# The end of a graph network kernel: gate written in place in PSUM, last weights loaded whole and split early, last tile in two pieces

## The chip, the cores and the metric

One core of a Trainium2 chip. The metric is device time in microseconds (us), the median of the runs shown. The core has five engines with queues of their own, which wait for each other by semaphores: TensorE (PE, matmuls; its weight loads are listed as PEld), VectorE (DVE), ScalarE (ACT), GpSimd (POOL) and SyncE (SP, which here issues all transfers). SBUF is the on-chip memory of 128 partitions, PSUM the eight banks of 512 fp32 columns into which PE writes.

## The reference

625 nodes with 1024 features, 20,000 edges of 8 types. A graph attention layer, a residual and a layer norm give x1; a relational layer with a gate, a residual and a second layer norm follow. What matters here is the end of the second layer:

```python
u = _rgcn(x, edge_index, edge_type, weight, root, bias)      # x @ root + bias + sum over r of mean_r @ weight[r]
z = jnp.concatenate([u, x], axis=1) @ w_gate + b_gate        # w_gate: 2048 x 1024
h = jnp.tanh(u) * z + x * (1.0 - z)
return h                                                     # and outside: layernorm(x + h)
```

With h rewritten, x + h = 2x + (tanh(u) - x) * z, and this is how both kernels compute it.

## The kernel before

The nodes are cut into five tiles of 128 rows (`NT`, the last has 113), the features into eight chunks of 128 (`KT`) and two halves of 512 columns (`H2`). All products are done in split precision: each fp32 operand is a high part (rounded to fp32r) and a low part (what is left), and each product is three matmuls, high x high, low x high, high x low. So 8 chunks x 5 tiles x 3 = 120 matmuls of 512 columns make one product, called a segment. Segments are numbered: `SEG_Z` (x1's part of z), `SEG_U` and the following 18 (root and the eight relations, two halves each), and then four for u's part of z, of which `SEG_G` is the left half's last one and `SEG_G + 1` the right half, of which all chunks use u.

Weights come chunk by chunk through a ring of four buffers (`RING`): SP loads `w_raw`, ACT rounds it to `w_hi`, POOL subtracts to get `w_lo`, and PE multiplies. `w_used` and `u_ready` tell ACT that a slot is free again. In the loop over relations this runs a few chunks ahead of PE.

The end: for `SEG_G - 1` and `SEG_G` PE goes chunk by chunk, all five tiles per chunk (`product_item`), and in the first two chunks of each it transposes u (`turn_u`), which ACT (`turned_u`) and DVE split into `M_hi[1]` and `M_lo[1]`. These are the transposed u of four chunks each. POOL meanwhile computes `xf` = x1 from its two parts. The last segment goes tile by tile instead, all eight chunks of a tile in turn, so that each tile is ready early; for this all eight chunks of the weights must be there at once. They are put into the memory of `M_hi[0]` and `M_lo[0]` (`last_w`), which is free when `SEG_G - 1` has been used. Their raw parts still come through the ring of four.

ACT then computes tanh of u in place, POOL subtracts xf from it (`minus_x`), and DVE runs `gate` for each tile and half: z += the product (L928), z *= tanh(u) - x (L931), u = 2 xf + z (L932), statistics (L933). In the second half each tile is then normalized: statistics aggregated (L940), square root on ACT (L653), reciprocal (L942), scaling (L943), and SP sends the tile out. The banks of the last segment are 5, 6, 7, 0, 1 for tiles 0 to 4 (`last_bank`), those of `SEG_G` 0 to 4, so tiles 3 and 4 wait for drained banks. The order on each engine is the order in which the code is written.

Of the kernel before, what the change touches and what calls it, by code (L numbers as in the profile page):

```python
# [5 lines left out]
def gat_rgcn_kernel(nc, dst_cols, src_cols, type_cols, dst_units, xT, x, weights, a, bias, b_gate, counts_dram, out):  # L6
    f32 = mybir.dt.float32
    f32r = mybir.dt.float32r
# [42 lines left out]
    GB = 3  # L51
    SUMS = 2 * KT

    def rows(t):
        return P if t < NT - 1 else N - P * (NT - 1)
# [4 lines left out]
    with ctx:  # L60
        def sem(name):
            return ctx.enter_context(nc.semaphore(name))

        def sb(name, shape, dt, where=ctx):
            return where.enter_context(nc.sbuf_tensor(name, shape, dt))
# [14 lines left out]
        stats = sb("stats", [P, NT, 2, 6], f32)  # L80
        y_sum = sb("y_sum", [P, NT], f32)
# [52 lines left out]
        with ExitStack() as late:  # L134
            x1_hi = sb("x1_hi", [P, NT, D], f32r, late)
            x1_lo = sb("x1_lo", [P, NT, D], f32r, late)
            u = sb("u", [P, NT, D], f32, late)
            z = sb("z", [P, NT, D], f32, late)
# [3 lines left out]
            with ExitStack() as agg:  # L142
                C_hi = sb("C_hi", [P, NT, NP], f32r, agg)
            xf = sb("xf", [P, NT, D], f32, late)

        g_parts = [m[:, :, :].rearrange("p a b -> p (a b)") for m in (M_hi[0], M_lo[0])]

        def last_w(low, k):
            return g_parts[low][:, k * H2:(k + 1) * H2]
# [93 lines left out]
        d_done = sem("d_done")  # L243
# [21 lines left out]

        ALL = KT * NT
# [28 lines left out]
        def _(sp):  # L295
# [75 lines left out]
            for n in range(SEG_U + 2 * R, SEG_G + 2):  # L371
                load_ahead(n, last=n == SEG_G + 1)
# [11 lines left out]
        def _(pool):  # L384
# [17 lines left out]
            def last_chunk(k):  # L402
                pool.wait_ge(w_hi_done, 8 * (SEG_G + 1) + k + 1)
                pool.tensor_tensor(last_w(1, k), w_raw[k % RING][:, :], last_w(0, k).bitcast(f32),
                                   ALU.subtract).then_inc(w_lo_done, 1)

            def minus_x(t):
                r = slice(0, rows(t))
                pool.wait_ge(tanh_done, t + 1)
                pool.wait_ge(xf_done, t + 1)  # L410
                pool.tensor_tensor(u[r, t, :], u[r, t, :], xf[r, t, :], ALU.subtract).then_inc(d_done, 1)  # L411
# [42 lines left out]
        def _(act):  # L454
# [165 lines left out]
            def last_chunk(k):  # L620
                act.wait_ge(raw_here[k % RING], 32 * (SEG_G + 1) + 16 * (k // RING) + 16)
                if k == 0:
                    act.wait_ge(u_ready, filled(SEG_G - 1))
                nc.scalar.copy(last_w(0, k), w_raw[k % RING][:, :]).then_inc(w_hi_done, 1)
# [8 lines left out]
            for kh in range(2):  # L633
                n = SEG_G - 1 + kh
                split_chunk(n, RING)
                for t in range(GB):
                    turned_u(t, kh)
                split_chunk(n, RING + 1)
                for t in range(GB, NT):
                    turned_u(t, kh)  # L640
                for k in range(RING + 2, KT):
                    split_chunk(n, k)
                if kh == 0:
                    for k in range(RING):
                        split_chunk(n + 1, k)
            for k in range(KT):
                last_chunk(k)
                if k < NT:
                    act.wait_ge(uT_lo_done, 2 * NT)
                    nc.scalar.activation(u[0:rows(k), k, :], u[0:rows(k), k, :], ACT.Tanh).then_inc(tanh_done, 1)  # L650
            for t in range(NT):
                act.wait_ge(var_done, t + 1)
                nc.scalar.activation(rstd[0:rows(t), t:t + 1], mv[0:rows(t), t, 1:2], ACT.Sqrt,  # L653
                                     bias=eps_col[0:rows(t), :]).then_inc(std2_done, 1)
# [3 lines left out]
        def _(dve):  # L658
# [265 lines left out]

            def gate(t, half, from_bank):
# [11 lines left out]
            for t in range(NT):  # L937
                r = slice(0, rows(t))
                gate(t, 1, last_bank(t))
                v.bn_aggr(mv[r, t, :], stats[r, t, :, :]).then_inc(var_done, 1)  # L940
                dve.wait_ge(std2_done, t + 1)
                step(v.reciprocal(rstd[r, t:t + 1], rstd[r, t:t + 1]))  # L942
                v.tensor_scalar(u[r, t, :], u[r, t, :], mv[r, t, 0:1], rstd[r, t:t + 1], ALU.subtract, ALU.mult)\  # L943
                    .then_inc(y2_done, 1)
# [3 lines left out]
        def _(pe):  # L948
# [247 lines left out]
            for t in range(NT):  # L1196
                if t >= GB:
                    pe.wait_ge(u_drained, NT * SEG_G + t - GB + 1 + NT)
                c, o = slice(t * P, t * P + rows(t)), bank(last_bank(t), rows(t))
                for k in range(KT):  # L1200
                    if t == 0:
                        pe.wait_ge(w_lo_done, 8 * (SEG_G + 1) + k + 1)
                    mm(o, M_hi[1][:, k, c], last_w(0, k), start=k == 0, stop=False)  # L1203
                    mm(o, M_lo[1][:, k, c], last_w(0, k), start=False, stop=False)  # L1204
                    last = mm(o, M_hi[1][:, k, c], last_w(1, k), start=False, stop=k == KT - 1)  # L1205
                last.then_inc(u_ready, 1)
# [42 lines left out]
```

## Time and profile before

| what | value |
|---|---|
| time, median of 3 runs | 1109.0 us (1108.06 to 1109.21) |
| the profiled execution | 1109.11 us, its span 1107.3 us |
| PE busy | 1042.9 us (94%), granted clock 0.977 of full speed on average |
| DVE, ACT, POOL busy | 344.8, 275.4, 265.8 us |
| last segment on PE | starts at 1060.77 us, 120 matmuls |
| weights loads | 192 of 256 KB, 2.9 us from issue to landing |
| a count matrix, C_hi<-C_dram | 1600 KB, 7.4 us from issue to landing |

The span is the time from the first to the last instruction of the profiled execution; times in the rows are counted from its start. A matmul's duration overlaps with the next one's, so distances between starts tell its cost. [...]

### The profile page before, as it was taken

The numbers are of one execution on the slowest core, as the hardware profiler recorded it, in microseconds if no ns is written. First come the engines' busy times: TensorE is split into PE (matmuls) and PEld (weight loads), VectorE is DVE, ScalarE is ACT, GpSimd is POOL, SyncE is SP. The second block draws the span as 40 slices with busy tenths as digits, with TensorE's granted clock in tenths as the row PEclk, the third lists the DMA queues.
The fourth block names the chain that finished last, engine by engine and source line by source line (L and its number), as shares of the span: only waits on it lengthen the run. The fifth ranks groups of instructions, "written<-read, shape, count | busy, mean of one in ns | idle before, by whom it ended". The sixth has DMA issues, their size and how long they took to land.

```text
span 1107.3 us, 14903 instructions
## 1 busy us (share of the span) xinstructions
PE 1042.9 (94%) x5430; PEld 857.2 (77%) x5430; DVE 344.8 (31%) x694; ACT 275.4 (25%) x470; POOL 265.8 (24%) x201
## 2 busy tenths in 40 slices
PE   5899879996999999999999999999999999999977
PEld 3566546775889889879889879889889889888855
DVE  7976765360112202202202102102102202112277
ACT  4322343383112212212212211211212211212320
POOL 0000000106331321221321321321321321327480
PEclk9999999998999999999999999999999998999989
DMA  6213335407321041041141141141141140212212
GB/s 209 76 39 108 94 96 152 133 28 262 122 76 39 30 147 37 29 146 37 31 145 38 29 146 30 38 145 34 33 146 38 30 147 28 75 48 67 76 39 92
DMA packets 63622, 91.81 MB, mean 83 GB/s; under 512 B 4116, under 2 KB 30179, under 8 KB 63429
## 3 DMA queue, kind: packets, MB, share of 16 engines
q1 hardware_dynamic: 63556, 90.86, 26.4%
q8 instruction: 51, 0.84, 0.3%
q14 instruction: 15, 0.11, 0.0%
HBM read 75.17 MB, written 15.67 MB: 82 GB/s over the span
## 4 chain that ended last, share of the span: by engine, by line
PE 84%; DVE 7%; POOL 3%; issue 3%; ACT 2%; DVEq 1%; DMA 0%; SPq 0%; ACTq 0%; POOLq 0%
PE ps L966 18%; PE ps L968 17%; PE ps L967 17%; PE ps L1154 9%; PE ps L1155 9%; PE ps L1030 4%; PE ps L993 2%; PE ps L1143 2%; DVE hot L790 2%; DVE oh_s L722 2%; POOL x_lo L426 1%; PE ps L1203 1%; POOL u L411 1%; PE ps L1205 1%; PE ps L1204 1%
## 5 line engine op out<-in xcount | busy, mean ns | idle before, releaser
L399 POOL TENSOR_TENSOR w_lo<-w_raw,w_hi 128x512 fp32r<-128x512 f32 x168 | 215.8, 1288 | 761.7 <-ACT w_hi L465 562.7
L966 PE MATMUL ps<-w_hi,M_hi 128*128 128x512 f32 (+1 forms) x560 | 223.4, 399 | 17.4 <-POOL w_lo L399 9.4
L465 ACT CAST w_hi<-w_raw 128x512 fp32r<-128x512 f32 x184 | 114.4, 622 | 498.2 <-PE ps L968 430.8
L968 PE MATMUL ps<-w_lo,M_hi 128*128 128x512 f32 (+1 forms) x560 | 219.7, 392 | 0.0
L967 PE MATMUL ps<-w_hi,M_lo 128*128 128x512 f32 (+1 forms) x560 | 219.7, 392 | 0.0
L883 DVE SCALAR_TENSOR_TENSOR u<-ps,scale,u 128x512 f32<-128x512 f32 (+1 forms) x90 | 66.4, 744 | 427.7 <-PE ps L968 427.7
L1154 PE MATMUL ps<-C_hi,x_hi 128*128 128x320 f32 (+3 forms) x640 | 194.0, 320 | 0.0
L1155 PE MATMUL ps<-C_hi,x_lo 128*128 128x320 f32 (+3 forms) x640 | 193.0, 318 | 0.0
L966 PE MATMUL ps<-w_hi,M 128*128 128x512 f32 (+1 forms) x360 | 142.9, 397 | 0.0
L967 PE MATMUL ps<-w_hi,M 128*128 128x512 f32 (+1 forms) x360 | 142.6, 396 | 0.0
L968 PE MATMUL ps<-w_lo,M 128*128 128x512 f32 (+1 forms) x360 | 142.3, 395 | 0.0
L966 PEld LDWEIGHTS ps<-w_hi,M_hi 128*128 128x128 f32 (+1 forms) x560 | 104.7, 187 | 43.5 <-POOL w_lo L399 9.9
L1154 PEld LDWEIGHTS ps<-C_hi,x_hi 128*128 128x128 f32 (+1 forms) x640 | 128.1, 200 | 0.4
L1155 PEld LDWEIGHTS ps<-C_hi,x_lo 128*128 128x128 f32 (+1 forms) x640 | 128.1, 200 | 0.4
L968 PEld LDWEIGHTS ps<-w_lo,M_hi 128*128 128x128 f32 (+1 forms) x560 | 104.6, 187 | 24.2
L967 PEld LDWEIGHTS ps<-w_hi,M_lo 128*128 128x128 f32 (+1 forms) x560 | 105.0, 187 | 22.2
L790 DVE TENSOR_SCALAR hot<-table,key 128x640 bf16<-128x640 f16 x210 | 69.6, 382 | 53.9 <-PE ps L1030 52.4
L1030 PE MATMUL ps<-hot,oh_s 128*128 128x320 bf16 x420 | 72.2, 301 | 12.4 <-DVE hot L790 5.7
L968 PEld LDWEIGHTS ps<-w_lo,M 128*128 128x128 f32 (+1 forms) x360 | 67.0, 186 | 17.5
L966 PEld LDWEIGHTS ps<-w_hi,M 128*128 128x128 f32 (+1 forms) x360 | 66.9, 186 | 16.7
L967 PEld LDWEIGHTS ps<-w_hi,M 128*128 128x128 f32 (+1 forms) x360 | 66.7, 185 | 16.6
L1030 PEld LDWEIGHTS ps<-hot,oh_s 128*128 x420 | 29.6, 97 | 43.3 <-issue 35.7
(145 smaller groups left out, 773.2 us busy)
## 6 DMA issues: line engine op xcount, KB each, us to landing
w_raw<-weights SPq DMA_DIRECT2D x192, 256.0 KB, 2.9
C_dram<-Cst SPq DMA_DIRECT2D x25, 512.0 KB, 6.0
C_hi<-C_dram SPq DMA_DIRECT2D x8, 1600.0 KB, 7.4
z<-b_gate SPq DMA_DIRECT2D x5, 512.0 KB, 9.8
u<-bias SPq DMA_DIRECT2D x5, 512.0 KB, 7.6
xT_raw<-xT SPq DMA_DIRECT2D x8, 312.5 KB, 7.5
u<-x SPq DMA_DIRECT2D x4, 512.0 KB, 5.2
out<-u SPq DMA_DIRECT2D x4, 512.0 KB
```

The costliest lines, as they stand in the source:

```text
L399: pool.tensor_tensor(w_lo[k % RING][:, :], w_raw[k % RING][:, :], w_hi[k % RING][:, :].bitcast(f32), ALU.subtract).then_inc(w_lo_done, 1)
L465: nc.scalar.copy(w_hi[k % RING][:, :], w_raw[k % RING][:, :]).then_inc(w_hi_done, 1)
L722: v.tensor_tensor(oh_s[:, t0 * P:t1 * P].rearrange("p (t s) -> p t s", s=P), iota_s[:, :].unsqueeze(1).broadcast_to([P, n, P]), src_h[:, t ...
L790: v.tensor_scalar(hot[:, SLOT[s] * NP:(SLOT[s] + 1) * NP], table[:, :], float(WIN * w), key[:, ds(tile + s, 1)], ALU.add, ALU.is_equal).th ...
L883: v.scalar_tensor_tensor(u[r, t, half * H2:(half + 1) * H2], bank(t, rows(t)), scale[odd][r, t:t + 1], u[r, t, half * H2:(half + 1) * H2], ...
L966: mm(o, lhs_hi[:, k, c], w_hi[k % RING][:, :], start=opens, stop=False)
L967: mm(o, lhs_lo[:, k, c], w_hi[k % RING][:, :], start=False, stop=False)
L968: last = mm(o, lhs_hi[:, k, c], w_lo[k % RING][:, :], start=False, stop=closes_)
L993: last = mm(bank(turn_bank(j, part), c0=(m - m0) * P, c=P), Cst[j % 2][:, m, r, :], ident_r[:, :], start=r == 0, stop=r == R - 1)
L1030: last = mm(bank(5 + c, c=SPLIT), oh_s[:, ds(edge + s * P, P)], hot[:, SLOT[s] * NP + c * SPLIT:SLOT[s] * NP + (c + 1) * SPLIT], start=Fal ...
L1154: mm(o, x1_hi[r, m, f], C_hi[r, m, c0:c0 + cn], start=m == 0, stop=False)
L1155: last = mm(o, x1_lo[r, m, f], C_hi[r, m, c0:c0 + cn], start=False, stop=m == NT - 1)
```

## The change

- Memory is laid out anew: `C_hi`, free memory and `x1_lo` lie together; `xf` takes the place of the first, and eight buffers `last_raw` take that of `x1_lo`.
- SP waits until all five xf are done, then loads the eight last chunks into `last_raw`, two at a time, each pair followed by one of the four last ordinary chunks.
- ACT and POOL split the last chunks between the ordinary ones. tanh of tiles 0 and 1 comes between, of 2 to 4 behind.
- x is subtracted by DVE instead of POOL, for all five tiles ahead of the gate.
- The gate is three operations: two write their result back into the PSUM bank, the third reads it and writes u, with an accumulator for the row sum. The statistics operation is gone for tiles 0 to 3; their mean is made from the row sums, and ACT squares u - mean with an accumulator, ahead of the root.
- Tile 4 of the last segment is done in two pieces of 256 columns in two banks, and its gate in four quarters, with the statistics operation as before.

```diff
@@ kernel memory
         with ExitStack() as late:
-            x1_hi = sb("x1_hi", [P, NT, D], f32r, late)
-            x1_lo = sb("x1_lo", [P, NT, D], f32r, late)
...
+            with ExitStack() as agg:
+                C_hi = sb("C_hi", [P, NT, NP], f32r, agg)
+                space = sb("space", [P, NT * (D - NP)], f32, agg)
+                x1_lo = sb("x1_lo", [P, NT, D], f32r, agg)
...
             xf = sb("xf", [P, NT, D], f32, late)
+            last_raw = [sb(f"last_raw{k}", [P, H2], f32, late) for k in range(KT)]
+            space2 = sb("space2", [P, NT * D - KT * H2], f32, late)
...
+            x1_hi = sb("x1_hi", [P, NT, D], f32r, late)
@@ SP
-            for n in range(SEG_U + 2 * R, SEG_G + 2):
-                load_ahead(n, last=n == SEG_G + 1)
+            for n in range(SEG_U + 2 * R, SEG_G):
+                load_ahead(n)
+            sp.wait_ge(xf_done, NT)
+            for k in range(KT):
+                r0, c0 = chunk_rows(SEG_G + 1, k)
+                sp.dma_start(last_raw[k][:, :], weights[ds(r0, P), c0:c0 + H2]).then_inc(last_here[k], 16)
+                if k % 2 == 1:
+                    load_chunk(SEG_G, RING + k // 2)
@@ POOL
-            for k in range(KT):
-                if k < RING:
-                    split_chunk(SEG_G, k + RING)
-                else:
-                    last_chunk(k - RING)
-                if k >= KT - NT:
-                    minus_x(k - KT + NT)
-            for k in range(RING, KT):
+            split_chunk(SEG_G, RING)
+            for k in range(3):
                 last_chunk(k)
+            split_chunk(SEG_G, RING + 1)
+            for k in range(3, 5):
+                last_chunk(k)
+            split_chunk(SEG_G, RING + 2)
+            for k in range(5, 7):
+                last_chunk(k)
+            split_chunk(SEG_G, RING + 3)
+            last_chunk(7)
@@ ACT, behind the chunks of SEG_G - 1
+            for k in range(RING + 1):
+                split_chunk(SEG_G, k)
+            for k in range(2):
                 last_chunk(k)
-                if k < NT:
-                    act.wait_ge(uT_lo_done, 2 * NT)
-                    nc.scalar.activation(u[0:rows(k), k, :], u[0:rows(k), k, :], ACT.Tanh).then_inc(tanh_done, 1)
...
+            for t in range(GB):
+                turned_u(t, 1)
+            last_chunk(2)
+            split_chunk(SEG_G, RING + 1)
+            for t in range(GB, NT):
+                turned_u(t, 1)
+            last_chunk(3)
+            last_chunk(4)
+            split_chunk(SEG_G, RING + 2)
+            last_chunk(5)
+            tanh(0)
+            tanh(1)
+            last_chunk(6)
+            split_chunk(SEG_G, RING + 3)
+            last_chunk(7)
+            for t in range(2, NT):
+                tanh(t)
+            for t in range(NT - 1):
+                r = slice(0, rows(t))
+                act.wait_ge(h_mean_done, t + 1)
+                nc.scalar.activation(z[r, t, :], u[r, t, :], ACT.Square, bias=h_neg_mean[r, t:t + 1],
+                                     accum_out=h_sq[r, t:t + 1]).then_inc(h_sq_done, 1)
+                act.wait_ge(h_sq_done, t + 1)
+                nc.scalar.activation(rstd[r, t:t + 1], h_sq[r, t:t + 1], ACT.Sqrt, bias=eps_col[r, :], scale=1.0 / D)\
+                  .then_inc(std2_done, 1)
@@ DVE
+            def gated(o, r, t, c):
+                step(v.tensor_tensor(o, o, z[r, t, c], ALU.add))
+                step(v.tensor_tensor(o, o, u[r, t, c], ALU.mult))
+
             def gate(t, half, from_bank):
...
-                v.tensor_tensor(z[r, t, c], bank(from_bank, rows(t)), z[r, t, c], ALU.add).then_inc(u_drained, 1)
+                o = bank(from_bank, rows(t))
+                gated(o, r, t, c)
+                v.scalar_tensor_tensor(u[r, t, c], xf[r, t, c], 2.0, o, ALU.mult, ALU.add,
+                                       accum_out=h_sum[r, t, half:half + 1]).then_inc(u_drained, 1)
                 dve.wait_ge(u_drained, NT * (SEG_G + half) + t + 1 + NT)
-                dve.wait_ge(d_done, t + 1)
-                step(v.tensor_tensor(z[r, t, c], z[r, t, c], u[r, t, c], ALU.mult))
-                step(v.scalar_tensor_tensor(u[r, t, c], xf[r, t, c], 2.0, z[r, t, c], ALU.mult, ALU.add))
-                step(v.bn_stats(stats[r, t, half, :], u[r, t, c]))
+            def gate_quarter(q, from_bank, from_col):
...
+                gated(o, r, t, c)
+                step(v.scalar_tensor_tensor(u[r, t, c], xf[r, t, c], 2.0, o, ALU.mult, ALU.add))
+                step(v.bn_stats(quarters[r, q, :], u[r, t, c]))
...
             for t in range(NT):
+                minus_x(t)
+            for t in range(NT - 1):
                 gate(t, 0, t)
-            for t in range(NT):
+            for q in range(2):
+                gate_quarter(q, NT - 1, q * Q)
+            dve.sem_inc(u_drained, 1)
+            for t in range(NT - 1):
                 r = slice(0, rows(t))
                 gate(t, 1, last_bank(t))
+                v.tensor_scalar(h_neg_mean[r, t:t + 1], h_sum[r, t, 1:2], h_sum[r, t, 0:1], -1.0 / D, ALU.add, ALU.mult)\
+                 .then_inc(h_mean_done, 1)
+                normalized(t, h_neg_mean[r, t:t + 1], ALU.add)
@@ PE, last segment
+                pieces = [(0, H2)] if t < NT - 1 else [(0, Q), (Q, H2)]
+                for f0, f1 in pieces:
+                    if f0 > 0:
+                        pe.wait_ge(u_drained, NT * SEG_G + t - GB + 2 + NT)
+                    o = bank(last_bank(t) + (f0 > 0), rows(t), c=f1 - f0)
```

VectorE's order in the second half of a middle tile, before:

```order
L928 TENSOR_TENSOR z<-ps,z 128x512 [waits u_ready]
L931 TENSOR_TENSOR z<-z,u 128x512 [waits d_done,u_drained]
L932 SCALAR_TENSOR_TENSOR u<-xf,z 128x512 [waits dve_step]
L933 BN_STATS stats<-u 128x6 [waits dve_step]
L940 BN_AGGR mv<-stats 128x2 [waits dve_step]
L942 RECIPROCAL rstd<-rstd 128x1 [waits std2_done]
L943 TENSOR_SCALAR u<-u,mv,rstd 128x1024 [waits dve_step]
```

and now:

```order
L966 TENSOR_TENSOR ps<-ps,z 128x512 [waits u_ready]
L967 TENSOR_TENSOR ps<-ps,u 128x512 [waits dve_step]
L974 SCALAR_TENSOR_TENSOR u,h_sum<-xf,ps 128x512 [waits dve_step]
L1006 TENSOR_SCALAR h_neg_mean<-h_sum 128x1 [waits u_drained]
L993 RECIPROCAL rstd<-rstd 128x1 [waits std2_done]
L994 TENSOR_SCALAR u<-u,h_neg_mean,rstd 128x1024 [waits dve_step]
```

The wait for POOL's difference (`d_done`) and the two statistics operations are gone; the wait for ACT's root stands behind the mean.

ScalarE's order from the eighth chunk of `SEG_G` and the last weights on, before (`raw_here` is a landed chunk of the ring):

```order
L465 CAST w_hi<-w_raw 128x512 [waits w_used,raw_here3]
L624 CAST M_hi<-w_raw 128x512 [waits u_ready,raw_here0]
L650 ACT_TABLE_LOAD
L650 ACTIVATE u<-u 128x1024 [waits uT_lo_done]
L624 CAST M_hi<-w_raw 128x512 [waits raw_here1]
...
L624 CAST M_hi<-w_raw 128x512 [waits raw_here3]
L653 ACT_TABLE_LOAD
L653 ACTIVATE rstd<-mv,eps_col 128x1 [waits var_done] x4
L653 ACTIVATE rstd<-mv,eps_col 113x1 [waits var_done]
```

and now, from the chunk before it on:

```order
L478 CAST w_hi<-w_raw 128x512 [waits w_used,raw_here2]
L637 CAST M_hi<-last_raw 128x512 [waits last_here5]
L640 ACT_TABLE_LOAD
L640 ACTIVATE u<-u 128x1024 x2
L637 CAST M_hi<-last_raw 128x512 [waits last_here6]
L478 CAST w_hi<-w_raw 128x512 [waits w_used,raw_here3]
L637 CAST M_hi<-last_raw 128x512 [waits last_here7]
L640 ACTIVATE u<-u 128x1024 x2
L640 ACTIVATE u<-u 113x1024
L681 ACTIVATE z,h_sq<-u,h_neg_mean 128x1024 [waits h_mean_done]
L684 ACT_TABLE_LOAD
L684 ACTIVATE rstd<-h_sq,eps_col 128x1 [waits h_sq_done]
```

Six of the last chunks' copies now stand ahead of the eighth ordinary chunk or between it and tanh, and the second table load moved from ahead of the first wait to behind the first square.

## Rows read from the trace of the kernel before

**Rows 1.** The page's chain that ended last, share of the span by engine.

```profile
PE 84%; DVE 7%; POOL 3%; issue 3%; ACT 2%; DVEq 1%; DMA 0%; SPq 0%; ACTq 0%; POOLq 0%
```

**Rows 2.** Timeline of PE, last segment: start, duration, instruction, idle before and its releaser.

```profile
1060.77 0.40 PE L1203 MATMUL ps<-M_hi,M 128*128 128x512 f32 x1
...
1066.42 0.79 PE L1203 MATMUL ps<-M_hi,M 128*128 128x512 f32 x1 [3.39 <-POOL M_lo L404]
...
1070.87 0.80 PE L1203 MATMUL ps<-M_hi,M 128*128 128x512 f32 x1 [2.80 <-POOL M_lo L404]
...
1078.03 0.39 PE L1203 MATMUL ps<-M_hi,M 128*128 128x512 f32 x1
...
1085.06 0.40 PE L1203 MATMUL ps<-M_hi,M 128*128 128x512 f32 x1
```

**Rows 3.** Window: busy PE, PEld, DVE, ACT, POOL, then clock, DMA share, GB/s.

```profile
1070.00:1077.00 7.00, 6.09 (x14) 3.84 (x15) 6.79 (x7) 1.90 (x2) 5.43 (x4) 0.55 0.00 0
```

**Rows 4.** Timeline of POOL, the first subtraction and the last four splits.

```profile
1050.58 2.41 POOL L411 TENSOR_TENSOR u<-u,xf 128x1024 f32<-128x1024 f32 x1 [1.60 <-ACT u L650]
...
1069.09 6.33 POOL L404 TENSOR_TENSOR M_lo<-w_raw,M_hi 128x512 fp32r<-128x512 f32 x4
```

**Rows 5.** Timeline of VectorE in the gate and at the end.

```profile
1058.15 0.69 DVE L928 TENSOR_TENSOR z<-ps,z 128x512 f32<-128x512 f32 x1 [16.64 <-PE ps L968]
1058.88 1.90 DVE L931 TENSOR_TENSOR z<-z,u 128x512 f32<-128x512 f32 x1
...
1083.33 0.81 DVE L943 TENSOR_SCALAR u<-u,mv,rstd 128x1024 f32<-128x1024 f32 x1
1084.05 0.69 DVE L928 TENSOR_TENSOR z<-ps,z 128x512 f32<-128x512 f32 x1
...
1102.19 0.21 DVE L940 BATCH_NORM_AGGREGATE mv<-stats 113x2 f32<-113x12 f32 x1
1102.77 0.16 DVE L942 RECIPROCAL rstd<-rstd 113x1 f32<-113x1 f32 x1 [0.36 <-ACT rstd L653]
1102.96 0.81 DVE L943 TENSOR_SCALAR u<-u,mv,rstd 113x1024 f32<-113x1024 f32 x1
```

**Rows 6.** Timeline of ScalarE around the last weights and tanh.

```profile
1043.49 0.62 ACT L465 CAST w_hi<-w_raw 128x512 fp32r<-128x512 f32 x1 [2.79 <-PE ps L968]
...
1048.15 1.28 ACT L650 ACT_TABLE_LOAD   x1
1049.45 1.06 ACT L650 ACTIVATE u<-u 128x1024 f32<-128x1024 f32 x1
```

**Rows 7.** Timeline of PE in the last aggregation, matmuls of 320 and of 306 columns.

```profile
962.37 0.31 PE L1154 MATMUL ps<-C_hi,x_hi 128*128 128x320 f32 x1
...
963.85 0.31 PE L1154 MATMUL ps<-C_hi,x_hi 128*128 128x306 f32 x1
```

**Rows 8.** VectorE by line and form: count, busy us, mean ns, idle before.

```profile
L883 DVE SCALAR_TENSOR_TENSOR u<-ps,scale,u 128x512 f32<-128x512 f32 x72 | 53.2, 745 | 427.7 <-PE ps L968 427.7
...
L896 DVE TENSOR_TENSOR M_lo<-ps,M_hi 128x320 fp32r<-128x320 f32 x32 | 15.8, 492 | 40.3 <-ACT M_hi L609 40.3
...
L747 DVE SCALAR_TENSOR_TENSOR M<-h_raw,a_bc 128x512 fp32r<-128x512 f32 x8 | 5.5, 686 | 0.0
...
L747 DVE DVE_READ_ACCUMULATOR M<-h_raw,a_bc 128x1 f32 x8 | 0.7, 84 | 0.0
```

**Rows 9.** Timeline of ScalarE in the first layer's norm.

```profile
234.88 1.15 ACT L569 ACTIVATE et<-u,neg_mean 128x1024 f32<-128x1024 f32 x1 [1.03 <-DVE neg_mean L840]
235.94 0.19 ACT L569 ACTIVATION_READ_ACCUMULATOR et<-u,neg_mean 128x1 f32 x1
...
237.44 0.30 ACT L574 ACTIVATE rstd<-y_sq,eps_col 128x2 f32<-128x2 f32 x1
```

**Rows 10.** Timeline of VectorE at the same place.

```profile
234.69 0.15 DVE L840 TENSOR_SCALAR neg_mean<-y_sum 128x1 f32<-128x1 f32 x1
...
237.77 0.17 DVE L844 RECIPROCAL rstd<-rstd 128x2 f32<-128x2 f32 x1 [0.66 <-ACT rstd L574]
```

More of the change, by code:

```diff
@@ L242, in gat_rgcn_kernel @@
         xf_done = sem("xf_done")
-        d_done = sem("d_done")
+        last_here = [sem(f"last_here{k}") for k in range(KT)]
+        last_hi_done = sem("last_hi_done")
+        last_lo_done = sem("last_lo_done")
+        h_mean_done = sem("h_mean_done")
+        h_sq_done = sem("h_sq_done")
         var_done = sem("var_done")
@@ L402, in last_chunk @@
             def last_chunk(k):
[L403 to L411, printed above, removed]
+                pool.wait_ge(last_hi_done, k + 1)
+                pool.tensor_tensor(last_w(1, k), last_raw[k][:, :], last_w(0, k).bitcast(f32),
+                                   ALU.subtract).then_inc(last_lo_done, 1)
             def split_ahead(n, last=False):
@@ L620, in last_chunk, with tanh @@
             def last_chunk(k):
-                act.wait_ge(raw_here[k % RING], 32 * (SEG_G + 1) + 16 * (k // RING) + 16)
+                act.wait_ge(last_here[k], 16)
                 if k == 0:
                     act.wait_ge(u_ready, filled(SEG_G - 1))
-                nc.scalar.copy(last_w(0, k), w_raw[k % RING][:, :]).then_inc(w_hi_done, 1)
+                nc.scalar.copy(last_w(0, k), last_raw[k][:, :]).then_inc(last_hi_done, 1)
+            def tanh(t):
+                nc.scalar.activation(u[0:rows(t), t, :], u[0:rows(t), t, :], ACT.Tanh).then_inc(tanh_done, 1)
             def turned_u(t, kh):
@@ L646, in _ @@
-            for k in range(KT):
-                last_chunk(k)
-                if k < NT:
-                    act.wait_ge(uT_lo_done, 2 * NT)
-                    nc.scalar.activation(u[0:rows(k), k, :], u[0:rows(k), k, :], ACT.Tanh).then_inc(tanh_done, 1)
-            for t in range(NT):
-                act.wait_ge(var_done, t + 1)
-                nc.scalar.activation(rstd[0:rows(t), t:t + 1], mv[0:rows(t), t, 1:2], ACT.Sqrt,
-                                     bias=eps_col[0:rows(t), :]).then_inc(std2_done, 1)
+            split_chunk(SEG_G - 1, RING)
@@ new lines, in _ @@
+            for t in range(GB, NT):
+                turned_u(t, 1)
[18 more added lines that the diff above has]
+                  .then_inc(std2_done, 1)
@@ L657, in _ @@
+            r = slice(0, rows(NT - 1))
+            act.wait_ge(var_done, 1)
+            nc.scalar.activation(rstd[r, NT - 1:NT], mv[r, NT - 1, 1:2], ACT.Sqrt, bias=eps_col[r, :]).then_inc(std2_done, 1)
         @block.vector
@@ L935, in _, with normalized @@
+            def normalized(t, mean, op):
+                r = slice(0, rows(t))
+                dve.wait_ge(std2_done, t + 1)
+                step(v.reciprocal(rstd[r, t:t + 1], rstd[r, t:t + 1]))
+                v.tensor_scalar(u[r, t, :], u[r, t, :], mean, rstd[r, t:t + 1], op, ALU.mult).then_inc(y2_done, 1)
             for t in range(NT):
+                minus_x(t)
+            for t in range(NT - 1):
                 gate(t, 0, t)
-            for t in range(NT):
+            for q in range(2):
+                gate_quarter(q, NT - 1, q * Q)
@@ L947, in _ @@
+            r = slice(0, rows(NT - 1))
+            for q in range(2, 4):
+                gate_quarter(q, last_bank(NT - 1) + q - 2, 0)
+            v.bn_aggr(mv[r, NT - 1, :], quarters[r, :, :]).then_inc(var_done, 1)
+            normalized(NT - 1, mv[r, NT - 1, 0:1], ALU.subtract)
         @block.tensor
@@ L1198, in _ @@
                     pe.wait_ge(u_drained, NT * SEG_G + t - GB + 1 + NT)
[L1199 to L1206, printed above, removed]
+                c = slice(t * P, t * P + rows(t))
+                pieces = [(0, H2)] if t < NT - 1 else [(0, Q), (Q, H2)]
[3 more added lines that the diff above has]
+                    o = bank(last_bank(t) + (f0 > 0), rows(t), c=f1 - f0)
+                    for k in range(KT):
+                        if t == 0:
+                            pe.wait_ge(last_lo_done, k + 1)
+                        mm(o, M_hi[1][:, k, c], last_w(0, k)[:, f0:f1], start=k == 0, stop=False)
+                        mm(o, M_lo[1][:, k, c], last_w(0, k)[:, f0:f1], start=False, stop=False)
+                        last = mm(o, M_hi[1][:, k, c], last_w(1, k)[:, f0:f1], start=False, stop=k == KT - 1)
+                    last.then_inc(u_ready, 1)
 def kernel(**inputs):
```

45 lines of the change are left out of this document (23 added, 22 removed).

## The prediction, made before the changed kernel ran

> **What bounds the kernel now.** I read the chain of waits first. Its shares by engine [rows 1] say that TensorE (PE) is the bound nearly throughout, so a change that touches only the end can give no more than what PE and the engines behind it lose there. Everything ahead of the last two products is issued in the same order by the changed program, so I took the timeline of the end next, engine by engine.
>
> PE issues one 512-column matmul every 0.2343 us (30 of them between 1078.03 and 1085.06 [rows 2]). It finishes its next-to-last product at 1060.77, where the last one begins, and should then need 120 x 0.2343 = 28.1 us. It takes until 1099.2. [...] POOL is late since its five subtractions of x, 2.4 us each and more, stand between the last splits, the last four of which end only at 1075.4 [rows 4].
>
> VectorE (DVE) starts the gate's first half at 1058.15 and ends the last tile at 1103.77 [rows 5] and the output's last transfer follows at once; the span ends at 1107.3, 3.5 us on. Those 3.5 us I leave as they are: tile 3 goes out some 5 us ahead of tile 4 before and after.
>
> **Part 1, the last weights.** They get memory of their own, which comes free when the five xf are computed. SP now waits for that (about 1025.4), then issues eight loads of 256 KB and, between them, the four last ordinary ones. Behind that wait on SP stand only these loads and the output. The first ordinary chunk among them is wanted by ACT at 1034.3, 9 us later. The queue holds 3 MB, for which an estimate from the 216 GB/s that the 1.6 MB of a count matrix in 7.4 us make (the table of the profile above) gives 14 us, so all are there by 1040; ACT takes the last at 1049. Covered with 9 us to spare.
>
> ScalarE (ACT) copies at 0.62 us [rows 6]: two now stand before three turned tiles of u, which come 1.1 us later (1035.9 rather than 1034.8). PE's fourth transposition, which needs the first of them back, begins at 1038.9; cover 1.7 us, cost nothing. After the copy released at 1043.49 [rows 6] ACT does one more, loads its table (1.28 [rows 6]), computes tanh of tiles 0 and 1 (1.06 each [rows 6]), then three copies and the other tanh, done about 1052.4. POOL's eight last splits (1.29 each, up to 1.74 beside VectorE) lie between its ordinary ones and end about 1053. PE asks for the first at 1060.77: 7 us cover. So both idle stretches and the slow clock go: four tiles of 24 matmuls end at 1060.77 + 22.5 = 1083.3.
>
> **Part 2, the last tile in two pieces.** 48 matmuls of 256 columns. The trace has 320 columns: ten in 1.48 us (962.37 to 963.85 [rows 7]). Through 0.148 and 0.2343 a line gives 0.119 at 256; bounds 0.117 (half of 512) and 0.148 (the 320 row). I take 0.119: 5.7 us, PE ends at 1089.0 (bounds 1088.9 to 1090.4). Its wait for three drained tiles is over by 1065.
>
> **Part 3, x subtracted by DVE.** An operation takes 0.492 us at 320 elements and 0.686 at 512 [rows 8], so 1.01 ns per element and 1.20 at 1024. Five of them can start at 1047.05 and take 6.0 us alone, but both their inputs lie in SBUF, and such an operation beside POOL took 1.90 for 0.69 [rows 5]. Between alone (1053.1, or 1053.6 behind the last tanh) and wholly beside POOL (5 x 2.5, 1059.6) I take 1056, since POOL has only three splits left then. The gate can't start before 1058.15, so the cost is 0 (bounds 0 and +1.5). POOL's 12.9 us of the same work disappear.
>
> **Part 4, the gate.** Before, a tile's half is four steps of 0.73 from start to start (1058.15 to 1058.88 [rows 5]). Now it is three, the last with an accumulator, of which the reading is a row of its own, 0.084 [rows 8]: 0.73 + 0.73 + 0.77 = 2.23. No row shows an operation that writes PSUM, and two of the three write there in place. Bounds: 0.05 cheaper, and for a dearer one the 745 ns of the row that reads PSUM in the relation steps against 0.69, +0.055 [rows 5, 8]. I take 0.69, what every quiet operation of 512 elements shows, wherever its input lies.
> [...]
>
> The DVE's own line, from 1058.15:
> - First halves of tiles 0 to 3: 4 x 2.23 = 8.9, to 1067.1.
> - Two quarters of tile 4, four steps each. A 256-element step by the same slope is 0.427, and a gap of 0.04, 0.467; 8 x 0.467 = 3.7, to 1070.8. PE has tile 0 ready at 1066.4, so DVE is already behind.
> - A second half: 2.23, then a wait that the old gate had not. It used statistics on DVE and waited 0.36 us for the root; now the mean goes to ACT, which squares 1024 elements. The same chain stands in the first layer [rows 9, 10]: mean start 234.69 to square start 234.88 is 0.19, 1.06 until the accumulator is read, 0.19 for that, a table load, and the root at 237.44, whose result starts the reciprocal at 237.77 (0.33). Without the table, and with a gap of 0.05: 1.82 from the mean to the reciprocal. Then 0.19 for the reciprocal and 0.72 for the scaling (1083.33 to 1084.05 [rows 5]). Sum 4.96.
> - Nothing on DVE is put into the wait; tile t+1's gate stands behind it. The first tile also pays the table: in ACT's order the load stands between square and root, where before it lay idle time ahead. 1.30 (the load's 1.28 [rows 6] and the gap to what follows).
> - Four tiles: 4 x 4.96 + 1.30 = 21.1, to 1091.9. Tile 3 is taken at 1087.0, PE had it at 1083.4: DVE sets the end, not PE, by 3.6 us there and 4.8 at the last piece.
> - Two quarters 3.7, then 0.58 from the aggregation to the reciprocal and 0.19 to the scaling, 0.81 [rows 5]: 1097.2.
> Against 1103.77 that is 6.5 us earlier. The profiled execution took 1109.1 (span 1107.3 and 1.8 outside it), so 1102.6; it lies 0.1 above the median of 1109.0, so I say 1102.5.
>
> **Rivals.**
> 1. PSUM steps dearer by a little. [...] For: no row of a PSUM write. Against: no cost of PSUM on the reading side. Chance 0.12.
> 2. In-place PSUM runs at half the rate, since each element is read and written in the same bank. Place: the first two steps of each gate. Price: 1.01 ns x 512 = 0.52 on 16 steps and 0.26 on 8: 10.4, nothing hides it as DVE is the bound: 1112.9, slower than before. It decides once such a step costs over 0.32 more. Against: the relation steps read a bank that quickly, and no row shows a rate that depends on the memory. Chance 0.04.
> 3. PE stays the bound. If DVE's line were 4.8 us shorter than my sum (wait on ACT shorter, PSUM steps cheaper), the end is PE's 1089.0 + 0.15 + 1.86 for a quarter + 1.58 tail = 1092.6: 1097.9. Against: every term but the write has its row. Chance 0.07.
> 4. The change doesn't do what it says: last weights late again, or the fourth transposition held up. The first 3.6 us of any PE delay are free behind DVE, so below that nothing is seen; with before's whole stall PE would end at 1099.3 and the last scaling at 1102.9, so 1108.2: even then not slower. Chance 0.04.
> 5. Something ahead of 1058, where memory was moved but no order: 0.03, either sign, within 0.2%.
>
> **How the numbers follow.** The forecast has 0.70 with its own range of 1101.0 to 1104.0. To that the range adds rival 1 with the page's figure, POOL beside the subtractions (+1.5), and downwards cheaper PSUM writes (24 x 0.05 = 1.2) with part of rival 3: 1099.8 to 1105.3. What a measurement here can tell from no change is 0.2%, 2.2 us: faster means below 1106.8. Cases 0 (own forecast), 1, 3 and 4 are faster: 0.93. Within 0.2%: 0.03. Slower: 0.04.
>
> **What would show it.** PE without idle time from 1060.8 to 1089, granted clock 1.00 throughout; the last splits done about 1053; DVE without idle time but for four waits of about 1.7 us (3.0 in the first) on ACT's root; last scaling ending about 1097. An in-place step over 0.8 us means rival 1 or 2; idle DVE waits on PE in the second halves mean rival 3; PE waits on POOL or an ACT copy, rival 4. Wrong altogether if the gate's first step starts well after 1058.2.

## The result, and the profile after

The changed kernel took 1099.4 us (median of 7 runs, 1093.9 to 1102.6) against 1109.0 (7 runs, 1106.5 to 1111.5): ratio 0.9911, 95% interval 0.9884 to 0.9938. It is faster, as forecast, but by 9.6 us where 6.5 were forecast, and lies 0.4 us outside the range. The profiled execution has a span of 1094.2 us, 13.1 less than before. Half of that is what the prediction summed up; the other half lies ahead of the place where its sum began.

**The end.** The timeline of VectorE in the changed kernel (start, duration, instruction, idle before it and its releaser), which answers to [rows 5]; its first line is the end of the subtractions, the second the gate's first step:

```profile
1043.94 5.70 DVE L963 TENSOR_TENSOR u<-u,xf 128x1024 f32<-128x1024 f32 x3 [1.03 <-ACT u L640]
1051.60 0.70 DVE L966 TENSOR_TENSOR ps<-ps,z 128x512 f32<-128x512 f32 x1 [1.95 <-PE ps L1037]
1052.33 0.70 DVE L967 TENSOR_TENSOR ps<-ps,u 128x512 f32<-128x512 f32 x1
1053.07 0.69 DVE L974 SCALAR_TENSOR_TENSOR u<-xf,ps 128x512 f32<-128x512 f32 x1
...
1060.38 0.43 DVE L966 TENSOR_TENSOR ps<-ps,z 113x256 f32<-113x256 f32 x1
...
1064.20 0.70 DVE L966 TENSOR_TENSOR ps<-ps,z 128x512 f32<-128x512 f32 x1 [0.15 <-DVE stats L988]
...
1069.53 0.16 DVE L993 RECIPROCAL rstd<-rstd 128x1 f32<-128x1 f32 x1 [2.92 <-ACT rstd L684]
...
1074.50 0.16 DVE L993 RECIPROCAL rstd<-rstd 128x1 f32<-128x1 f32 x1 [1.64 <-ACT rstd L684]
...
1085.37 0.43 DVE L966 TENSOR_TENSOR ps<-ps,z 113x256 f32<-113x256 f32 x1
...
1089.88 0.81 DVE L994 TENSOR_SCALAR u<-u,mv,rstd 113x1024 f32<-113x1024 f32 x1
```

| stretch on VectorE | forecast | measured |
|---|---|---|
| four first halves (1051.60 to 1060.38) | 8.9 | 8.78 |
| two quarters (to 1064.20) | 3.7 | 3.82 |
| four second halves with scaling (to 1085.37) | 21.1 | 21.17 |
| two quarters, root, scaling (to 1090.69) | 5.3 | 5.32 |
| sum | 39.05 | 39.09 |

Before, the same stretch was 45.62 us (1058.15 to 1103.77). An operation that reads and writes the same PSUM bank takes 0.70 us, as long as the undisturbed ones of 512 elements before (0.69), so the two rivals on PSUM are out. The waits on ScalarE's root are 2.92 us once, with the table's load (1.28 us, at 1067.91 in ScalarE's timeline), and 1.64 three times. TensorE, which answers to [rows 2]:

```profile
1054.13 0.39 PE L1277 MATMUL ps<-M_hi,M 128*128 128x512 f32 x1
...
1081.90 0.28 PE L1278 MATMUL ps<-M_hi,M 128*113 128x256 f32 x1
1082.02 0.28 PE L1279 MATMUL ps<-M_lo,M 128*113 128x256 f32 x1
```

It runs through from 1054.13 to 1082.3, 28.2 us as forecast, with a 256-column matmul every 0.12 us. GpSimd's last split ends at 1048.56, 5.6 us before the first of them:

```profile
1046.29 2.27 POOL L421 TENSOR_TENSOR M_lo<-last_raw,M_hi 128x512 fp32r<-128x512 f32 x1
```

**Where the 6.5 us come from.** Not mainly from TensorE's stall. In the timeline of VectorE before, the second halves start at 1079.65, and the only waits on TensorE in the gate are these two:

```profile
1079.65 0.69 DVE L928 TENSOR_TENSOR z<-ps,z 128x512 f32<-128x512 f32 x1
...
1093.69 0.69 DVE L928 TENSOR_TENSOR z<-ps,z 128x512 f32<-128x512 f32 x1 [0.76 <-PE ps L1205]
...
1099.29 0.69 DVE L928 TENSOR_TENSOR z<-ps,z 113x512 f32<-113x512 f32 x1 [1.10 <-PE ps L1205]
```

The first halves took 21.5 us before (1058.15 to 1079.65) since their operations with both inputs in SBUF took 1.28 to 1.90 us beside GpSimd and 0.69 behind its last split; in the changed kernel they take 12.6 (1051.60 to 1064.20), 8.9 less. From there to the end it is 2.4 us more (24.1 and 26.5). With first halves as slow as before, an end of the stall alone could have brought no more than the two waits, 1.9 us (an estimate from these rows).

**Ahead of the end.** The gate's first step stands at 1051.60 instead of 1058.15, 6.55 us that no term of the prediction has. The transfer of the counts, one in each relation step, dates the steps. Before, in the timeline of SyncE:

```profile
390.65 0.38 SPq L316 DMA_DIRECT2D C_hi<-C_dram  x1
...
640.71 0.38 SPq L316 DMA_DIRECT2D C_hi<-C_dram  x1
...
724.11 0.38 SPq L316 DMA_DIRECT2D C_hi<-C_dram  x1
```

and in the changed kernel:

```profile
387.52 0.38 SPq L327 DMA_DIRECT2D C_hi<-C_dram  x1
...
637.49 0.38 SPq L327 DMA_DIRECT2D C_hi<-C_dram  x1
...
719.26 0.38 SPq L327 DMA_DIRECT2D C_hi<-C_dram  x1
```

The step that begins at 640.71 before took 83.40 us, to 724.11, and its like in the changed kernel 81.77. Between 390 and 637 us the steps differ by under 0.25. The 1.6 us come from TensorE's clock. In each step 25 matmuls of two columns sum the counts' rows, and in seven of the eight steps before and four of the eight now a stretch of some 3.4 us at a granted clock of 0.50 follows them (339.0 to 342.4 us before is one), in one step of each kernel twice. The window around the first of these places, before and then after (columns as in [rows 3]: clock, DMA share and GB/s stand last):

```profile
336.00:346.00 10.00, 10.00 (x65) 10.00 (x65) 3.60 (x8) 1.89 (x4) 1.27 (x1) 0.83 0.17 50
```

```profile
334.00:344.00 10.00, 10.00 (x76) 9.95 (x75) 4.53 (x10) 2.30 (x5) 1.26 (x1) 1.00 0.18 55
```

A clock of 0.83 over 10 us is 1.7 us lost, and 65 matmuls were started instead of 76. A loss is counted here by the clock; the step that has it is some 1.6 us longer (83.3 against 81.7). Read in windows of 2 us, the profile of before has 8 such losses of 1.7 us between 330 and 930 us, that of the changed kernel 5. That makes 5.1 of the 6.55. Of the rest, 1.1 us lie in the first interval between count transfers, beyond its missing loss. A stretch of slow clock lies in it in both kernels, at 260 to 272 us before and at 256 to 268 now, where TensorE is busy 3.3 us of the 12 instead of 7.0, so it falls more on idle time; that this is the cause is likely and not shown.

### The profile page after: what moved, and what is told of

The parts are those of the page before. It is cut to its first block, busy times and chain, and to the rows that moved or that the text cites. A ratio compares the mean times of both kernels' runs of the same rounds, so it can differ in the third digit from the quotient of the medians.

```text
span 1094.2 us, 14960 instructions
## 1 busy us (share of the span) xinstructions
PE 1032.7 (94%) x5454; PEld 852.1 (78%) x5454; DVE 341.7 (31%) x707; ACT 279.6 (26%) x478; POOL 253.6 (23%) x196
## 4 chain that ended last, share of the span: by engine, by line
PE 83%; DVE 9%; issue 3%; ACT 3%; POOL 1%; DVEq 1%; DMA 0%; SPq 0%; ACTq 0%
PE ps L1035 18%; PE ps L1036 18%; PE ps L1037 18%; PE ps L1223 9%; PE ps L1224 9%; PE ps L1099 4%; PE ps L1062 2%; PE ps L1212 2%; DVE hot L824 2%; DVE oh_s L756 2%; POOL x_lo L437 1%; DVE ps L967 1%; DVE ps L966 1%; DVE w_lo L751 1%; PE ps L1070 1%
## 5 line engine op out<-in xcount | busy, mean ns | idle before, releaser
L1223 PE MATMUL ps<-C_hi,x_hi 128*128 128x320 f32 (+3 forms) x640 | 190.5, 315 | 0.0
L1224 PE MATMUL ps<-C_hi,x_lo 128*128 128x320 f32 (+3 forms) x640 | 189.4, 313 | 0.0
L1224 PEld LDWEIGHTS ps<-C_hi,x_lo 128*128 128x128 f32 (+1 forms) x640 | 125.4, 196 | 0.4
L1223 PEld LDWEIGHTS ps<-C_hi,x_hi 128*128 128x128 f32 (+1 forms) x640 | 125.3, 196 | 0.4
```

The source lines that it names most:

```text
L1223: mm(o, x1_hi[r, m, f], C_hi[r, m, c0:c0 + cn], start=m == 0, stop=False)
L1224: last = mm(o, x1_lo[r, m, f], C_hi[r, m, c0:c0 + cn], start=False, stop=m == NT - 1)
```

## The experiments

Was the number of slow stretches chance, or did the new layout change it? The first four kernels ask that. Ratios are against the kernel before, run beside them. The stretch from the gate's first step to the last scaling's end is called the end.

**The kernel before, unchanged.**

> The kernel before once more, unchanged. Theory A (chance): the 6.5 us that the changed kernel gained ahead of the gate are three stretches of slow clock fewer in the relation loop (8 episodes of 3.4 us at the low clock, 1.7 us lost each, against 5) and a better place of the one at 256 to 272 us; their number changes from run to run of the same kernel. Then this profile shows another number of episodes than 8 in the loop, and its time differs from 1109.1 by 1.7 us per episode, within 1104 to 1113. Theory B (layout): the number belongs to the kernel, 8 again, and times within 1 us of each other.

1108.1 us (12 runs, 1103.1 to 1112.7), ratio 0.9986 (0.9958 to 1.0015). The profile had 8 losses again, so the first sign that I had named did not come; but they lie in other steps (none near 506, two at 420 to 428). The 34 runs of the kernel before that stood beside these four kernels went from 1099.7 to 1115.1, which theory B, times within 1 us of each other, does not allow. So its times speak against B, and its number of losses does not tell.

**The new layout alone.** The kernel before with the memory block of the changed one; `last_raw` is there and unused.

```diff
-            x1_hi = sb("x1_hi", [P, NT, D], f32r, late)
-            x1_lo = sb("x1_lo", [P, NT, D], f32r, late)
...
+            with ExitStack() as agg:
+                C_hi = sb("C_hi", [P, NT, NP], f32r, agg)
+                space = sb("space", [P, NT * (D - NP)], f32, agg)
+                x1_lo = sb("x1_lo", [P, NT, D], f32r, agg)
...
+            x1_hi = sb("x1_hi", [P, NT, D], f32r, late)
```

> The kernel before with the changed kernel's memory layout and nothing else. Theory B (the new places of x1_hi, x1_lo and C_hi make the relation loop faster): 3 episodes fewer, time about 1102.5, ratio 0.994. Theory A (chance): the same distribution of times as the kernel before, ratio 1.000 within 0.002, gate starting anywhere from 1053 to 1060.

1104.9 us (12 runs, 1102.5 to 1111.3), ratio 0.9986 (0.9961 to 1.0011). The layout does nothing to the time that can be told from nothing, and theory B's 0.994 lies outside the interval. Its profile has 4 losses in the loop and its gate starts at 1053.36; that profile alone would have fitted B as well.

**The changed kernel, unchanged.**

> The changed kernel once more, unchanged. From the gate's first step to the last scaling both theories expect 39.1 us again, as this stretch has no slow clock and VectorE sets it. Theory A: the stretch ahead of the gate differs by 1.7 us per episode from 1051.6, ratio to the kernel before 0.989 to 0.994. Theory B: it is 1051.6 again and the ratio is 0.988.

1102.6 us (12 runs, 1094.4 to 1104.2), ratio 0.9942 (0.9918 to 0.9965). The end is 39.11 us again (1057.58 to 1096.69), but the gate starts 6 us later than in the first profile, with 6 losses in the loop and another slow stretch at 132 to 148, outside it. By the clock 6.8 us are lost there, of which 3.0 reach the first count transfer (247.96 instead of 244.98). The ratio is what was forecast for the change (0.994). That the time itself, 1102.6, is the forecast's too is partly luck, since the kernel before stood at 1107.6 beside it and not at 1109.0.

**Seven matmuls more ahead of the loop.**

```diff
+            for _ in range(7):
+                mm(bank(5), ident_r[:, :], M_hi[0][:, 0, 0:H2], start=True, stop=True)
             with pe.Fori(0, R // 2) as j:
```

> The changed kernel with seven matmuls of 512 columns more ahead of the relation loop, 7 x 0.2343 = 1.6 us of busy TensorE. If an episode depends on how the row-sum matmuls (25 of 2 columns in each step) lie to the clock's own beat, this shift changes which steps are hit: the time moves by +1.6 plus or minus 1.7 for each of several episodes, so anything from 1094 to 1106. If the episodes depend on the work alone, the same steps are hit as in the unchanged kernel and the time is 1.6 us longer, no more.

1102.5 us (11 runs, 1097.5 to 1108.6), ratio 0.9945 (0.9919 to 0.997); 6 losses in the loop. Since the unchanged kernel's own pattern varies as much, this tells nothing on what the shift does: inconclusive.

**Row sums of 100 columns.**

```diff
-                            last = mm(bank(5, c0=2 * t, c=2), C_hi[:, m, t * P:(t + 1) * P], ones_r[:, 0:2],
+                            last = mm(bank(5, c0=100 * t, c=100), C_hi[:, m, t * P:(t + 1) * P], ones_r[:, 0:100],
-                v.tensor_scalar(scale[1 - odd][:, :], bank(5, c=2 * NT).rearrange("p (t c) -> p t c", c=2)[:, :, 0],
+                v.tensor_scalar(scale[1 - odd][:, :], bank(5, c=100 * NT).rearrange("p (t c) -> p t c", c=100)[:, :, 0],
```

> The changed kernel, but each of the 25 row-sum matmuls per relation step multiplies by 100 columns of ones instead of 2 and one of the 100 equal sums is read. Theory A says that the slow stretches of the relation loop follow these matmuls of two columns, in which TensorE has almost nothing to stream; with 100 columns no episode is left between 330 and 930 us, some 7 x 1.7 = 12 us less than the same kernel without the edit (about 1102), so about 1091, and the spread of the runs shrinks from 10 us to under 5. Rival: the episodes come from elsewhere (the transfer of the count matrix, the waits ahead of the step); then their number stays at 5 to 8 and the time at 1094 to 1104. Cost of the wider matmuls: they are issued every 0.109 us, more than 100 columns need, so none.

1093.5 us (6 runs, 1088.3 to 1095.7), ratio 0.9871 (0.9838 to 0.9903). No loss is left in the loop. The time is 2.5 us above the forecast and the spread 7.4 us, not under 5, so the runs still differ by something; this profile has slow stretches only outside the loop. The granted clock of this one profile is recorded as 0.95 wherever it isn't lower, though its matmuls are no slower (one in 0.233 us at the end). The repetition below shows 1.00. The slow stretches of the loop belong to the two-column matmuls; why the clock falls behind them, and not in every step, no run tells.

**The old gate with the early weights.** The changed kernel with gate, statistics and root written as in the kernel before; VectorE's subtraction stays. The core of the edit:

```diff
-                gated(o, r, t, c)
-                v.scalar_tensor_tensor(u[r, t, c], xf[r, t, c], 2.0, o, ALU.mult, ALU.add,
-                                       accum_out=h_sum[r, t, half:half + 1]).then_inc(u_drained, 1)
+                v.tensor_tensor(z[r, t, c], bank(from_bank, rows(t)), z[r, t, c], ALU.add).then_inc(u_drained, 1)
...
+                step(v.tensor_tensor(z[r, t, c], z[r, t, c], u[r, t, c], ALU.mult))
+                step(v.scalar_tensor_tensor(u[r, t, c], xf[r, t, c], 2.0, z[r, t, c], ALU.mult, ALU.add))
+                step(v.bn_stats(stats[r, t, half, :], u[r, t, c]))
```

> The changed kernel with the gate of the kernel before (four steps of 0.73, statistics on VectorE, one bank for the last tile), the early last weights and VectorE's subtraction kept. My sum for VectorE from the gate's first step: 5 x 2.91 + 4 x 4.40 + 4.49 = 36.7 us to the last scaling's end, against 39.1 with the new gate: the early weights alone bring 9 us and the new gate takes 2.4 back (ACT's square and table load in VectorE's line). If instead the three-operation gate is what brings the time, this stretch is over 39.1.

1098.4 us (6 runs, 1094.6 to 1100.8), ratio 0.9918 (0.9888 to 0.9948). The end is 36.60 us (1056.10 to 1092.70), 2.5 shorter than with the new gate. The new gate costs time here, but not by its three operations: a half takes 2.20 us with it (1051.60 to 1053.80) and 2.90 with the old (1056.10 to 1059.00). What it costs is VectorE's wait for the square and the root, 1.64 us and 2.92 once, against 0.36 with the old statistics.

**Scaling behind the next gate.** Tile 3's scaling stands between the last two quarters.

```diff
                 gate(t, 1, last_bank(t))
...
-                normalized(t, h_neg_mean[r, t:t + 1], ALU.add)
+                if t > 0:
+                    normalized(t - 1, h_neg_mean[0:rows(t - 1), t - 1:t], ALU.add)
...
+                if q == 2:
+                    normalized(NT - 2, h_neg_mean[0:rows(NT - 2), NT - 2:NT - 1], ALU.add)
```

> The changed kernel with one edit of order: VectorE scales tile t only behind the gate of tile t+1, so that ACT's square and root run beside a gate. If VectorE's waits on ACT set the end, as my sum had it, TensorE becomes the bound: from the gate's first step to the last scaling's end 34.5 us instead of 39.1 (PE's end 30.9 after that step, 0.15, two quarters of 1.86 of which one lies behind PE, 1.58 of tail), idle VectorE before L966 released by PE. If the waits are hidden anyway, 39.1 stays.

1097.4 us (4 runs, 1094.6 to 1099.6), ratio 0.9904 (0.9868 to 0.994). The end is 34.62 us (1058.80 to 1093.42). In the timeline of VectorE the wait on ScalarE is nearly gone and waits on TensorE have come in:

```profile
1076.75 0.16 DVE L993 RECIPROCAL rstd<-rstd 128x1 f32<-128x1 f32 x1 [0.60 <-ACT rstd L684]
...
1083.93 0.70 DVE L966 TENSOR_TENSOR ps<-ps,z 128x512 f32<-128x512 f32 x1 [2.27 <-PE ps L1282]
```

So the same three operations, with the wait filled, end 2.0 us sooner than the old gate (34.62 and 36.60).

**The last tile in one piece.** The core of the edit; the last two quarters then read the halves of one bank.

```diff
-                pieces = [(0, H2)] if t < NT - 1 else [(0, Q), (Q, H2)]
+                pieces = [(0, H2)]
```

> The changed kernel with the last tile of the last segment in one piece of 512 columns, its gate still in quarters. VectorE comes to this tile 4.8 us behind TensorE, so the two pieces bring nothing: 39.1 us from the gate's first step to the last scaling's end, within 0.1. If the pieces are worth what they are for, half the last gate lies ahead of PE's end and this kernel is 1.9 us longer there.

1101.7 us (8 runs, 1096.9 to 1106.0), ratio 0.9946 (0.9922 to 0.9969). The end is 39.10 us (1052.51 to 1091.61): the two pieces are worth nothing while VectorE is behind.

**Wide row sums in the kernel before, in the changed one, and with the moved scaling.**

> The kernel before with row-sum matmuls of 100 columns instead of 2, nothing else. With the relation loop free of slow stretches its gate starts near 1047.6, as in the changed kernel with the same edit, and its end keeps the 45.6 us from the gate's first step to the last scaling: about 8 episodes x 1.7 = 13 us less than the kernel before, so 1095, or 1098 if some remain elsewhere. Rival (the layout or the early loads make the loop faster): the gate starts 3 us or more later than in the changed kernel with wide sums.

> The changed kernel with wide row sums again, on the same chip as the kernel before with wide sums. The change's own effect without the loop's noise: the end's 6.5 us, so the ratio between the two (each against the kernel before) is 0.994. If the loop were faster by the change itself, the ratio is 0.991 or less.

> The changed kernel with wide row sums and with scaling moved behind the next gate. The two gains lie in different places and add: 4.5 us less than with wide sums alone, about 1088, ratio 0.982, the fastest of all; 34.6 us from the gate's first step to the last scaling's end. If they do not add, TensorE's clock falls somewhere at the end and the stretch is over 36.

| kernel, wide sums | median of 6 runs | lowest to highest | ratio to the kernel before | gate starts | end |
|---|---|---|---|---|---|
| before | 1098.8 | 1096.6 to 1102.3 | 0.9919 (0.989 to 0.9949) | 1046.02 | 45.26 |
| changed | 1090.7 | 1089.6 to 1095.0 | 0.9846 (0.9817 to 0.9874) | 1046.07 | 39.10 |
| changed, moved scaling | 1087.8 | 1085.7 to 1091.5 | 0.9816 (0.9788 to 0.9845) | 1047.69 | 34.64 |

The relation loop of the first two, one line of windows each:

```profile
330.00:930.00 600.00, 596.22 (x3141) 517.56 (x3140) 111.72 (x211) 122.63 (x236) 148.79 (x116) 1.00 0.22 71
```

```profile
330.00:930.00 600.00, 595.48 (x3139) 516.61 (x3138) 111.78 (x211) 122.49 (x236) 148.76 (x116) 1.00 0.22 71
```

With the slow stretches out of the loop both gates start at the same time to 0.05 us, so in these two profiles the change does nothing ahead of it. The kernel before with two columns had 3077 matmuls in the same 600 us at a mean clock of 0.98. The row of 25 sums takes 2.89 us with 100 columns and 2.85 with two, so the wider ones cost next to nothing. The gate of the kernel before starts 12.1 us earlier in the profile, near the 13 forecast, but the median gains only 9.0 us (ratio 0.9919) and lies on the upper of the two values forecast: the profiled run is the fastest of the six, and the others show lower mean clocks (down to 0.980 against 0.990) in places that were not recorded. The profiled spans, 1094.8 and 1088.7, differ by 6.1 us, the ends by 6.16. The ratio of the two median times is 0.9926; six runs of each do not tell it from the 0.994 that the ends make, nor from the 0.991 of a faster loop; the gates' equal starts do. The third kernel is the fastest of all, by 2.9 us in the median and 4.5 in the end; its profile has one slow stretch more, at 134 to 146 us, which moves its gate and not its end.

**VectorE's subtraction alone.** In the kernel before, POOL no longer subtracts x, VectorE does ahead of the gate.

```diff
-                if k >= KT - NT:
-                    minus_x(k - KT + NT)
...
-                dve.wait_ge(d_done, t + 1)
...
+                step(v.tensor_tensor(u[r, t, :], u[r, t, :], xf[r, t, :], ALU.subtract))
```

> The kernel before with one part of the change: VectorE subtracts x, ahead of the gate, and GpSimd only splits; the last weights still come through the ring of four. Theory A: GpSimd's subtractions were the larger part of TensorE's stall, the ring the smaller. The last split then ends about 1062 instead of 1075.4, TensorE idles under 2 us or not at all, and the gate, delayed some 2 us by the subtractions beside GpSimd, ends 38 to 40 us after 1058: from PE's end of the next-to-last product's first tile to the last scaling's end some 39 instead of 45.6. Theory B: the ring of four is what made the weights late (ACT waited 12.5 us in all for four of the chunks); then TensorE still idles 4 us or more and the stretch stays over 43.

1102.2 us (10 runs, 1094.9 to 1109.7), ratio 0.9943 (0.9916 to 0.9969). TensorE has no idle time at the last segment any more, though the weights still come through the ring; the timeline of GpSimd has

```profile
1046.30 14.17 POOL L404 TENSOR_TENSOR M_lo<-w_raw,M_hi 128x512 fp32r<-128x512 f32 x7 [0.86 <-ACT M_hi L622]
```

so the last split ends at 1060.5. This kernel's next-to-last product runs 4.8 us earlier than in [rows 6] (the copy of 1043.49 is at 1038.70), so the 1062 of the expectation would be 1057.2: beside VectorE's subtractions a split takes 2.0 us instead of 1.29, and it is 3 us late without holding TensorE. In this profile TensorE is done with the next-to-last product's first tile about 1053.4 (11.2 us behind the copy at 1042.20, as before), and the last scaling ends at 1093.81: 40.4 us against 45.6, 5.2 gained. Theory A is right on TensorE's stall; the stretch is 1.4 us longer than its "some 39", and the gate starts 2.6 us late instead of some 2. The stall is not where most of the gain lies: VectorE's first halves, now hardly beside GpSimd, take 15.8 us (1055.96 to 1071.72) instead of 21.5, the rest of the gate 22.1 instead of 24.1, and the late start costs 2.6.

Together the profiles split the change's 6.5 us. Moving the subtraction brings 5.2, the early weights 3.7 more (40.4 against 36.7, which is the old gate's 36.60 and some 0.1 from TensorE's end to its first step), and the new gate takes 2.5 back.

## Why the prediction was wrong where it was

- **TensorE, 10.3 us of stall and slow clock gone (the two waits of [rows 2], the clock of [rows 3]); 0.119 us per matmul of 256 columns**: right. No idle time, clock 1.00, 28.2 us for the segment, 0.12 us per matmul of 256 columns. The last split was 5.6 us ahead of TensorE, not 7 or more: beside VectorE's subtraction it took 2.27 us, where at most 1.74 had been allowed. It cost nothing.
- **TensorE as what the end had lost by**: only in part, and without harm to the sum. VectorE waited 1.86 us for TensorE; its first halves, slowed beside GpSimd, had lost 7.0 us (21.5 instead of the 14.5 of the old gate with the early weights). The sum has that gain only because it takes every step at its quiet duration.
- **The subtraction on VectorE**: done at 1049.64, 1.95 us ahead of the gate; 2.1 had been forecast. Right; three of the five took 1.90 us each beside GpSimd, two 1.25.
- **The gate's steps, ACT's square and table load in VectorE's line, VectorE as the new bound**: right in each term to 0.15 us, 39.09 against 39.05, and shown by the moved scaling, which takes 4.5 us off and makes TensorE the bound. That the new gate gives time back (2.5 us) and that the pieces bring nothing follow from the same sum; the prediction did not say so, the later runs measured it.
- **The range's upper end, 1105.3**, holds with rival 1 a term for dearer operations on PSUM that no run shows. What the runs show in its place is 0.70 us for an operation that reads and writes PSUM in place, against 0.69 for one that reads PSUM and writes SBUF.
- **The step that failed is case 5**, "something ahead of 1058 ... 0.03, either sign, within 0.2%", and with it the 0.2% as what a measurement can tell. The first three runs of before lay within 1.2 us; 34 of the same kernel later spread over 15. I took one profiled execution's relation loop for the kernel's own, without asking how often its clock falls there: its losses of 1.7 us each were 4 to 8 in ten profiles with two-column sums, and 0 in four with 100 columns. The change's own effect is 6.2 to 6.5 us, the difference of the ends; the 3 us more in the median of seven runs are luck: measured again it was 6.4 us in all (ratio 0.9942), and with wide sums the loops of both kernels are equal. The two ratios' intervals overlap (0.9884 to 0.9938, 0.9918 to 0.9965), so this rests on the profiles, one execution each. The range of +-2.8 us was wide enough for the change and too narrow for a median of seven such runs.

Open is what decides in which steps the clock falls; the shifted kernel could not tell. Open too are the slow stretches outside the loop (132 to 154 and 256 to 278 us), which the wide sums left and no run varied.

## What to carry to other kernels

When a step takes one of two durations, here 83.4 and 81.8 us, look at the granted clock in short windows before comparing kernels, and take the effect from stretches that no slow clock touches. A row of tiny matmuls can cost time behind it: here 1.7 us at a time behind a row of 2.85. Making them wide cost next to nothing (2.89 us a row) and was worth 9 us in the kernel before (ratio 0.9919), more than the whole change. VectorE's waits on ScalarE (2.92 us once and 1.64 three times) went, but for one of 0.60, when the next tile's work was placed into them, and the end fell from 39.1 to 34.6 us; moving the statistics to ScalarE had brought these waits in (0.36 us before). An engine can be late because another slows its operations (here 7.0 us of VectorE's first halves) as well as because it waits; and a step that only shortens an engine that is ahead of the bound was worth nothing here (the end is 39.10 us without the pieces and 39.09 with them).

## What was not expected of the hardware

- Behind 25 matmuls of two columns, 2.9 us in all and without a gap, the granted clock fell to 0.50 for some 3.4 us in seven of eight steps (the profile of before; four of eight in that of the changed kernel), although TensorE was recorded as busy throughout (3.40 of the 3.40 us from 339.0 to 342.4).
- The granted clock of one execution stood at 0.95 through all its undisturbed stretches (the profile's mean is 0.937) without slower matmuls (one in 0.233 us, as at 1.00); its relation steps took 81.6 to 82.3 us, as the undisturbed ones at 1.00 do.
- The mean of the row sums (L1006) took 0.21 us, where that of the first layer took 0.15 [rows 10]. Both stand behind an accumulator; L1006 adds a second value from memory, L840 does not.
- VectorE's operations with both inputs in SBUF and GpSimd's took longer beside each other: up to 1.90 us instead of 0.69 for one of 512 elements, and up to 2.27 instead of 1.29 for a split.
